# Softmax row sums of an attention block: three joins before the sum product in place of two, and its place half a group later

## The chip, the core and the metric

One core of one Trainium2 chip runs the whole kernel. The metric is device time in microseconds (us) from launch to end. Several runs are taken of each kernel, and one execution of each is profiled.

## The reference

For x of 8 batches, 1024 tokens and 512 features, in float32:

```
x = x + attention(layernorm(x))      # 16 heads of 32 features, rotary part, low-rank q and kv of rank 256
x = x + mix(layernorm(x))            # r = sigmoid(xr Wr), k = relu(xk Wk)^2, out = r * (k Wv)

attn = einsum('bhqd,bhkd->bhqk', query, key) / scale
attn = softmax(attn, axis=-1)
out  = einsum('bhqk,bhkd->bhqd', attn, value)
```

The softmax is made of exp(score - row maximum), its product with the values (o) and its row sum (l). The kernel stores o and l apart, and the mix stage divides.

## The kernel before

Three stages run one after the other: a projection (it ends at about 690 us of the trace), the attention (`attend_block`, 690 to 2360 us) and the mix stage (`mix_block`, to the end). The change lies in `attend_block` alone.

The attention runs over 32 groups (`NG`), each one batch and four heads (`HG`). A group has two halves of 512 queries (`qc`), and a half has four units (`w` = 0 to 3), each of two key tiles: `u` counts the eight units of a group, and `h = 2n + qc` counts halves. Below, w0 to w3 are the four adds of a half that belong to its units, and w0' is that of the next half.

- TensorE: eight score products of a unit (L804, into the three PSUM banks `ps_s`), between them one maximum product each for the group that comes next (L264, read by VectorE at L280 with four banks, and transposed at L259), then the value product of the unit before (L817, 16 instructions). `sums` (L831) multiplies the joined exponentials with a block of ones, so that all 128 partitions are summed. Its result takes a turn of the same three banks `ps_s`; `place`, `l_place` and `L_AT` number these turns.
- ScalarE: eight exps of a unit into `probs` (L898), a ring of `PR` = 3 units. A unit's exps wait until the value product and GpSimd's add of the unit three before are done (L893, L895). It also copies o (L873) and l (L880) out of PSUM.
- GpSimd: one add for each unit joins its two key tiles in `pairs` (L922). After w1 it issues a transfer that adds pair 0 onto pair 1 (L926, an SBUF to SBUF transfer of 1 MB that accumulates in its destination). After w3 it adds pair 2 and pair 3 itself (L929). So two buffers are left for a half, `SUMMED = [1, 3]`, and `sums` runs 2 x 4 products for them. GpSimd waits at w1 and w3 until the sum products of the half before have read the buffer.
- SyncE: in order, `load_group` for the group two ahead once the last value product of the group before is done (ten loads, 3.5 MB), the stores of o and l, and `stack_max` (L289, L290), which puts the negated maxima into the stack of the next group.
- VectorE: the maxima (L280, L283, L277) and nothing else in this stage.

The order of every queue is written out by hand with semaphores: `joined` counts landed transfers, `pair_done` GpSimd's adds (`ADDS` = 5 for a half), `sum_done` the sum products, `exped` all that ScalarE has taken out of `ps_s`.

On TensorE, `sums` of half 0 of a group stands behind the value product in unit 5, and that of half 1 in unit 1 of the next group.

Of the kernel before, what the change touches and what calls it, by code (L numbers as in the profile page):

```python
# [21 lines left out]
ALU = mybir.AluOpType  # L22
# [5 lines left out]
HD = D // H  # L28
# [645 lines left out]
def attend_block(nc, sem, held, t, att, scratch, o_d, l_d):  # L674
# [9 lines left out]
    SR = 3  # L684
    PR = 3
    ADDS = ROUNDS + 1
    SUMMED = [1, 3]
    SUMS = len(SUMMED)
    RUN = TILES + NQ
    L_AT = 2 * UT  # L690
    HALF_RUN = ROUNDS * UT + 1
    assert RUN % SR == 0 and R3 * UNITS % PR == 0

# [17 lines left out]
    with ExitStack() as ctx:  # L711
        def sb(name, shape, dt=F32):
            return ctx.enter_context(nc.sbuf_tensor(name, shape, dt))
# [3 lines left out]
        qs, ks, vt, ones = att["q"], att["k"], att["v"], att["ones"]  # L717
        loaded, v_loaded, m_scored, m_read, m_stacked = (att[k] for k in ("loaded", "v_loaded", "m_scored", "m_read", "m_stacked"))
        probs = sb("probs", [P, PR, KB, HG, CH])
        pairs = sb("pairs", [P, ROUNDS, HG, CH])  # L720
        o_sb = sb("o_sb", [P, NQ, CH])
        l_sb = sb("l_sb", [P, NQ, CH])
        ps_s = [ctx.enter_context(nc.psum_tensor(f"ps_s{i}", [P, CH], F32)) for i in range(SR)]
# [6 lines left out]
        pv_done = sem("pv_done")  # L730
        pair_done = sem("pair_done")
        joined = sem("joined")
        sum_done = sem("sum_done")
        o_out = sem("o_out")
        o_stored = [sem(f"o_stored{q}") for q in range(NQ)]
# [56 lines left out]
        @block.tensor  # L792
        def _(pe):
            def scores(n, r, u, x):
                qc, w = divmod(u, ROUNDS)
                a, kt = x % HG, w * KB + x // HG
                v = place(u * UT + x)
                if u == 0 and x == 0 and type(n) is int and n == 1:
                    pe.wait_ge(rows_set, 16 * (R3 - 1))
                if w == 0 and x == 0:  # L800
                    pe.wait_ge(m_stacked[qc], 16 * (n + 1))
                if v >= SR or not is_first(n):
                    pe.wait_ge(exped, taken(n, v - SR))
                nc.tensor.matmul(ps_s[v % SR][:, :], ks[r][:, a, kt * P:(kt + 1) * P],  # L804
                                 qs[r][:, qc, a, :], start=True, stop=True).then_inc(scored, 1)

            def pv(n, i, r, u):
                qc, w = divmod(u, ROUNDS)
                if u == 0:
                    pe.wait_ge(v_loaded[r], 16 * (i + 1))  # L810
                if w == 0 and not (is_first(n) and qc == 0):
                    pe.wait_ge(o_out, n * NQ + qc)
                pe.wait_ge(exped, taken(n, place(u * UT + UT - 1)))
                for k in range(KB):
                    kt = w * KB + k
                    for a in range(HG):
                        m = nc.tensor.matmul(ps_o[a * HD:(a + 1) * HD, :], vt[r][:, kt, a * HD:(a + 1) * HD],  # L817
                                             probs[:, (r * UNITS + u) % PR, k, a, :], start=kt == 0, stop=kt == KT - 1)
                m.then_inc(pv_done, 1)

            def sums(n, qc):

                v = l_place(n, qc)
                pe.wait_ge(exped, taken(n, v - SR))
                for k, w in enumerate(SUMMED):
                    if k == 0:
                        pe.wait_ge(joined, 16 * (n * NQ + qc + 1))
                    else:
                        pe.wait_ge(pair_done, (n * NQ + qc + 1) * ADDS)
                    for a in range(HG):  # L830
                        m = nc.tensor.matmul(ps_s[v % SR][a * HD:(a + 1) * HD, :], ones[:, :], pairs[:, w, a, :],  # L831
                                             start=k == 0, stop=k == SUMS - 1)
                    m.then_inc(sum_done, 1)

            def step(i, r, n):


                r1 = (r + 1) % R3
                i1 = i + 1 if r1 == 0 else i
                todo = [] if is_last(n) else list(range(STEPS))  # L840
                spread = SPREAD_FIRST if is_first(n) else SPREAD

                def maxima(count):
                    for _ in range(count if todo else 0):
                        max_product(nc, pe, att, ps_m, t["ident"], n + 1, r1, i1 + 1, todo.pop(0))

                for u in range(UNITS):
                    for x in range(UT):
                        maxima(spread[u][x])
                        scores(n, r, u, x)  # L850
                    if u >= 1:
                        pv(n, i, r, u - 1)
                        if u == ROUNDS + 1:
                            sums(n, 0)
                        if u == 1 and not is_first(n):
                            sums(n - 1, 1)
                    elif not is_first(n):
                        pv(n - 1, i if r else i - 1, (r - 1) % R3, UNITS - 1)
                    maxima(spread[u][UT])
                if is_last(n):  # L860
                    pv(n, i, r, UNITS - 1)
                    sums(n, 1)

            pe.wait_ge(att["ones_done"], 1)
            rounds(step)

        @block.scalar
        def _(act):
            def take_o(n, qc):
                act.wait_ge(pv_done, n * UNITS + (qc + 1) * ROUNDS)  # L870
                if not is_first(n):
                    act.wait_ge(o_stored[qc], 16 * n)
                nc.scalar.copy(o_sb[:, qc, :], ps_o[:, :]).then_inc(o_out, 1)  # L873

            def take_l(n, qc):
                v = l_place(n, qc)
                act.wait_ge(sum_done, (n * NQ + qc + 1) * SUMS)
                if not is_first(n):
                    act.wait_ge(l_stored[qc], 16 * n)
                nc.scalar.copy(l_sb[:, qc, :], ps_s[v % SR][:, :]).then_inc(exped, 1)  # L880

            def step(i, r, n):
                for u in range(UNITS):
                    if u == ROUNDS + 1:
                        take_o(n, 0)
                    if u == ROUNDS + 2:
                        take_l(n, 0)
                    if u == 1 and not is_first(n):
                        take_o(n - 1, 1)
                    if u == 2 and not is_first(n):  # L890
                        take_l(n - 1, 1)
                    if u >= PR or not is_first(n):
                        act.wait_ge(pv_done, n * UNITS + u - PR + 1)  # L893
                        qc, w = divmod(u - PR, ROUNDS)
                        act.wait_ge(pair_done, (n * NQ + qc) * ADDS + w + 1)  # L895
                    for x in range(UT):
                        act.wait_ge(scored, n * TILES + u * UT + x + 1)
                        nc.scalar.activation(probs[:, (r * UNITS + u) % PR, x // HG, x % HG, :], ps_s[place(u * UT + x) % SR][:, :],  # L898
                                             ACT.Exp, scale=SCALE).then_inc(exped, 1)
                if is_last(n):  # L900
                    take_o(n, 1)
                    take_l(n, 1)

            rounds(step)

        @block.gpsimd
        def _(pool):
            def step(i, r, n):
                for u in range(UNITS):
                    qc, w = divmod(u, ROUNDS)  # L910
                    h = n * NQ + qc
                    if not (is_first(n) and qc == 0):
                        if w == 0:
                            pool.wait_ge(joined, 16 * h)
                        elif w == 1:
                            pool.wait_ge(sum_done, (h - 1) * SUMS + 1)
                        elif w == 2:
                            pool.wait_ge(pair_done, h * ADDS)
                        else:
                            pool.wait_ge(sum_done, h * SUMS)  # L920
                    pool.wait_ge(exped, taken(n, place(u * UT + UT - 1)))
                    nc.gpsimd.tensor_tensor(pairs[:, w, :, :], probs[:, (r * UNITS + u) % PR, 0, :, :], probs[:, (r * UNITS + u) % PR, 1, :, :],  # L922
                                            ALU.add).then_inc(pair_done, 1)
                    if w == 1:
                        pool.wait_ge(pair_done, h * ADDS + 2)
                        nc.gpsimd.dma_start(pairs[:, 1, :, :], pairs[:, 0, :, :], accum_op=ALU.add).then_inc(joined, 16)  # L926
                    if w == 3:
                        pool.wait_ge(pair_done, h * ADDS + 4)
                        nc.gpsimd.tensor_tensor(pairs[:, 3, :, :], pairs[:, 2, :, :], pairs[:, 3, :, :],  # L929
                                                ALU.add).then_inc(pair_done, 1)  # L930

            rounds(step)

# [589 lines left out]
```

## Time and profile before

| | us |
|---|---|
| median of 3 runs | 3187.87 (3184.89 to 3192.63) |
| the profiled execution | 3185.31 |
| its span, first to last instruction | 3183.5 |
| mean granted TensorE clock | 0.982 |

| engine, whole span | busy us | share |
|---|---|---|
| TensorE | 3038.1 | 95% |
| VectorE | 2193.7 | 69% |
| GpSimd | 2096.1 | 66% |
| ScalarE | 1488.2 | 47% |

The shares are means over three stages. In the page's slices, GpSimd is at 9 tenths or more all through the attention and at 0 to 1 in the projection, so its 66% says little; the stage has to be read alone. In the trace PE is TensorE's matmul row and PEld its weight load, DVE is VectorE, ACT ScalarE, POOL GpSimd and SP SyncE. The records of the ones product are 16 for a half (fp32 products appear as two each).

### The profile page before, as it was taken

To read this page: it belongs to the slowest core of one execution; us is meant where nothing else is said; L and a number is where in the kernel's file an instruction comes from. 1 tells how busy PE (TensorE), PEld (TensorE's weight loads), DVE (VectorE), ACT (ScalarE), POOL (GpSimd) and SP (SyncE) were. 2 spreads that over 40 slices of the span, in tenths; PEclk is the share of its full clock that TensorE was granted. 3 is DMA by queue.
4 is the path that set the end of the run, shared out by engine and by line. 5 is a ranking of instruction groups with operands and counts; after the bars stand their busy time and mean duration, and the time that the engine had idled before them with its cause. 6 is when DMAs were issued, how large, how long until landed. Compare 5 with 4: busy or idle time off the path is not lost. (4 is left out here: it accounts for less than half of the span.)

```text
span 3183.5 us, 42900 instructions
## 1 busy us (share of the span) xinstructions
PE 3038.1 (95%) x15508; PEld 2030.9 (64%) x15508; DVE 2193.7 (69%) x3337; ACT 1488.2 (47%) x2714; POOL 2096.1 (66%) x718
## 2 busy tenths in 40 slices
PE   7999999989999999999999999999957999999998
PEld 4888888855555555555555555555515877778776
DVE  3454544568777777777777777777708787787784
ACT  1222222226666666666666666666643233233232
POOL 0111111118999999999999999999964666566663
PEclk8999999989999999999999999999988999999999
DMA  3455454655556564646455565646243223323321
GB/s 103 159 177 180 159 176 164 192 142 115 123 119 134 118 136 105 143 98 146 107 134 120 120 132 118 137 107 143 51 123 103 84 76 105 87 71 105 94 64 40
DMA packets 189068, 382.84 MB, mean 120 GB/s; under 512 B 17105, under 2 KB 53105, under 8 KB 180721
## 3 DMA queue, kind: packets, MB, share of 16 engines
q1 hardware_dynamic: 179696, 313.70, 35.8%
q0 software_dynamic: 9216, 67.11, 10.3%
q8 instruction: 93, 1.52, 0.2%
q14 instruction: 63, 0.51, 0.1%
HBM read 194.59 MB, written 118.49 MB: 98 GB/s over the span
## 5 line engine op out<-in xcount | busy, mean ns | idle before, releaser
L280 DVE TENSOR_REDUCE part_max<-ps_m 128x1 f32<-128x512 f32 x1984 | 1211.9, 681 | 362.2 <-PE ps_m L264 362.1
L922 POOL TENSOR_TENSOR pairs<-probs 128x2048 f32<-128x2048 f32 x256 | 1181.9, 4619 | 170.4 <-ACT probs L898 135.6
L898 ACT ACTIVATE probs<-ps_s 128x512 f32<-128x512 f32 x2048 | 1036.7, 625 | 324.5 <-PE ps_s L804 308.4
L264 PE MATMUL ps_m<-k_stack,q_stack 96*128 96x512 f32 x1984 | 816.0, 412 | 40.2 <-DVE neg_max L277 34.0
L804 PE MATMUL ps_s<-q_stack,k_stack 97*128 97x512 f32 x2048 | 817.0, 402 | 5.9 <-PEq L313 4.0
L264 PEld LDWEIGHTS ps_m<-k_stack,q_stack 96*128 96x128 f32 x1984 | 376.9, 190 | 306.4 <-DVE part_max L280 136.9
L817 PE MATMUL ps_o<-probs,v_tiles 128*32 128x512 f32 x4096 | 494.0, 600 | 0.0
L804 PEld LDWEIGHTS ps_s<-q_stack,k_stack 97*128 97x128 f32 x2048 | 387.7, 190 | 137.8 <-ACT probs L898 21.2
L548 POOL TENSOR_TENSOR y_cos<-y_rot,cos 64x512 f32<-64x512 f32 x16 | 20.5, 1284 | 474.6 <-DVE y_swap L644 474.6
L929 POOL TENSOR_TENSOR pairs<-pairs 128x2048 f32<-128x2048 f32 x64 | 293.2, 4581 | 5.0
L817 PEld LDWEIGHTS ps_o<-probs,v_tiles 128*32 128x32 f32 x4096 | 107.1, 109 | 231.5 <-issue 175.7
L1288 POOL TENSOR_TENSOR gate<-gate,xs 128x512 f32<-128x512 f32 x64 | 115.2, 1802 | 132.3 <-DVE diff L1354 114.7
L1208 ACT ACTIVATE relu<-mix_p 128x512 f32<-128x512 f32 x64 | 38.3, 598 | 236.6 <-PE mix_p L1106 181.6
L1104 PE MATMUL mix_p<-mix_w_o_hi,o_hi 128*128 128x512 f32 x256 | 102.9, 402 | 41.0 <-DVE o_lo L1398 28.2
L1372 DVE TENSOR_TENSOR ka_lo<-relu,ka_hi 128x512 fp32r<-128x512 f32 x64 | 104.3, 1629 | 47.9 <-ACT ka_hi L1202 45.6
L1257 POOL TENSOR_TENSOR xs<-mix_x_in,bo 128x512 f32<-128x512 f32 x64 | 117.2, 1835 | 25.7 <-DMA mix_x_in<-in_x 21.3
L831 PE MATMUL ps_s<-pairs,ones 128*32 128x512 f32 x1024 | 122.7, 596 | 5.8 <-POOL pairs L929 5.8
L880 ACT COPY l_sb<-ps_s 128x512 f32<-128x512 f32 x64 | 37.6, 587 | 183.7 <-PE ps_s L831 183.7
L1346 DVE SCALAR_TENSOR_TENSOR mixed<-diff,mu_k,xT 128x512 f32<-128x512 f32 x64 | 112.3, 1795 | 0.6
L621 DVE TENSOR_TENSOR st_v<-ps_p,bv 128x512 f32<-128x512 f32 x64 | 44.2, 691 | 98.1 <-PE ps_p L450 98.1
L1275 POOL TENSOR_TENSOR relu<-relu 128x512 f32<-128x512 f32 x64 | 68.7, 1083 | 64.4 <-ACT relu L1208 64.4
L1104 PE MATMUL mix_p<-mix_w_v_hi,ka_hi 128*128 128x512 f32 x256 | 102.5, 400 | 8.2 <-DVE ka_lo L1372 8.0
(179 smaller groups left out, 4791.8 us busy)
## 6 DMA issues: line engine op xcount, KB each, us to landing
pairs<-pairs POOLq DMA_DIRECT2D x64, 1024.0 KB, 8.0
q_stack<-q_hi_scratch SPq DMA_DIRECT2D x128, 256.0 KB, 6.2
k_stack<-k_hi_scratch SPq DMA_DIRECT2D x64, 512.0 KB, 10.8
x_in<-in_x SPq DMA_DIRECT2D x16, 1024.0 KB, 5.5
q_hi_scratch<-st_hi SPq DMA_DIRECT2D x64, 256.0 KB, 2.3
q_lo_scratch<-st_lo SPq DMA_DIRECT2D x64, 256.0 KB, 2.5
k_hi_scratch<-st_hi SPq DMA_DIRECT2D x64, 256.0 KB, 2.4
k_lo_scratch<-st_lo SPq DMA_DIRECT2D x64, 256.0 KB, 2.7
```

Of the source, the lines that this page charges most:

```text
L264: nc.tensor.matmul(bank[:, :], att["q"][r][0:ROWS, half, h, q * P:(q + 1) * P], att["k"][r][0:ROWS, h, kc * CH:(kc + 1) * CH], start=True, ...
L280: nc.vector.reduce_max(part_max[:, half, j, kc:kc + 1], bank[:, :], AX).then_inc(att["m_read"], 1)
L804: nc.tensor.matmul(ps_s[v % SR][:, :], ks[r][:, a, kt * P:(kt + 1) * P], qs[r][:, qc, a, :], start=True, stop=True).then_inc(scored, 1)
L817: m = nc.tensor.matmul(ps_o[a * HD:(a + 1) * HD, :], vt[r][:, kt, a * HD:(a + 1) * HD], probs[:, (r * UNITS + u) % PR, k, a, :], start=kt ...
L831: m = nc.tensor.matmul(ps_s[v % SR][a * HD:(a + 1) * HD, :], ones[:, :], pairs[:, w, a, :], start=k == 0, stop=k == SUMS - 1)
L898: nc.scalar.activation(probs[:, (r * UNITS + u) % PR, x // HG, x % HG, :], ps_s[place(u * UT + x) % SR][:, :], ACT.Exp, scale=SCALE).then_ ...
L922: nc.gpsimd.tensor_tensor(pairs[:, w, :, :], probs[:, (r * UNITS + u) % PR, 0, :, :], probs[:, (r * UNITS + u) % PR, 1, :, :], ALU.add).th ...
L929: nc.gpsimd.tensor_tensor(pairs[:, 3, :, :], pairs[:, 2, :, :], pairs[:, 3, :, :], ALU.add).then_inc(pair_done, 1)
L1104: nc.tensor.matmul(out, stat_hi(f), mov_hi(f), start=f == 0, stop=False)
L1257: nc.gpsimd.tensor_tensor(xs[par][:, s, :], x_in[:, s, :], bo[:, :], ALU.add).then_inc(xb_done, 1)
L1288: nc.gpsimd.tensor_tensor(gate[:, s, :], gate[:, s, :], xs[par][:, s, :], ALU.add).then_inc(out_done, 1)
L1346: v = nc.vector.scalar_tensor_tensor(mixed[:, f, :], diff[:, f, :], mu_k[:, f:f + 1], prev[:, f, :], ALU.mult, ALU.add)
```

## The change

For each half, the joins become a chain into a buffer of its own, `full`, of which there are two (`FULL`), used in turn by the halves:

- w0 writes pair 0, w1 writes into `full`, and GpSimd itself adds pair 0 onto `full` right behind w1 (it was a transfer).
- After w2 GpSimd issues a transfer that adds `pairs` 1 (the third pair) onto `full` (`joined`).
- After w0' of the next half it issues a second transfer that adds `pairs` 2 (the fourth pair) onto `full` (`filled`). It waits for `joined` before it, and at the last half it stands right behind w3.
- `sums` waits for `filled` and runs 4 products in place of 8. It stands in unit 7 (half 0) and in unit 3 of the next group (half 1), two units later than before.
- ScalarE copies l of half 0 ahead of unit 0 of the next group, and that of half 1 ahead of unit 4; SyncE's stores of l follow it. In the last group l of half 0 is copied after the last exps.
- The waits of GpSimd for `sum_done` go to one, at w1, for the half two before.

```diff
-    SUMMED = [1, 3]
-    SUMS = len(SUMMED)
+    SUMS = 1
+    FULL = 2
-    L_AT = 2 * UT
+    L_AT = 4 * UT
-        pairs = sb("pairs", [P, ROUNDS, HG, CH])
+        pairs = sb("pairs", [P, ROUNDS - 1, HG, CH])
+        full = sb("full", [P, FULL, HG, CH])
...
-                for k, w in enumerate(SUMMED):
-                    if k == 0:
-                        pe.wait_ge(joined, 16 * (n * NQ + qc + 1))
-                    else:
-                        pe.wait_ge(pair_done, (n * NQ + qc + 1) * ADDS)
-                    for a in range(HG):
-                        m = nc.tensor.matmul(ps_s[v % SR][a * HD:(a + 1) * HD, :], ones[:, :], pairs[:, w, a, :],
-                                             start=k == 0, stop=k == SUMS - 1)
-                    m.then_inc(sum_done, 1)
+                pe.wait_ge(filled, 16 * (n * NQ + qc + 1))
+                for a in range(HG):
+                    m = nc.tensor.matmul(ps_s[v % SR][a * HD:(a + 1) * HD, :], ones[:, :], full[:, (n * NQ + qc) % FULL, a, :],
+                                         start=True, stop=True)
+                m.then_inc(sum_done, 1)
...
-                        if u == ROUNDS + 1:
+                        if u == ROUNDS + 3:
                             sums(n, 0)
-                        if u == 1 and not is_first(n):
+                        if u == 3 and not is_first(n):
                             sums(n - 1, 1)
...
-                        act.wait_ge(pair_done, (n * NQ + qc) * ADDS + w + 1)
+                        act.wait_ge(pair_done, (n * NQ + qc) * ADDS + [1, 2, 4, 5][w])
...
+            def add_last_pair(h):
+                pool.wait_ge(pair_done, h * ADDS + 5)
+                pool.wait_ge(joined, 16 * h + 16)
+                nc.gpsimd.dma_start(full[:, h % FULL, :, :], pairs[:, 2, :, :], accum_op=ALU.add).then_inc(filled, 16)
...
+                    acc = full[:, h % FULL, :, :]
+                    into = [pairs[:, 0, :, :], acc, pairs[:, 1, :, :], pairs[:, 2, :, :]][w]
+                    if h >= 1:
                         if w == 0:
+                            pool.wait_ge(pair_done, h * ADDS)
+                        elif w == 1 and h >= FULL:
+                            pool.wait_ge(sum_done, h - FULL + 1)
+                        elif w == 2:
                             pool.wait_ge(joined, 16 * h)
+                        elif w == 3:
+                            pool.wait_ge(filled, 16 * h)
...
+                    if w == 0 and h >= 1:
+                        add_last_pair(h - 1)
                     if w == 1:
                         pool.wait_ge(pair_done, h * ADDS + 2)
-                        nc.gpsimd.dma_start(pairs[:, 1, :, :], pairs[:, 0, :, :], accum_op=ALU.add).then_inc(joined, 16)
-                    if w == 3:
+                        nc.gpsimd.tensor_tensor(acc, pairs[:, 0, :, :], acc, ALU.add).then_inc(pair_done, 1)
+                    if w == 2:
                         pool.wait_ge(pair_done, h * ADDS + 4)
-                        nc.gpsimd.tensor_tensor(pairs[:, 3, :, :], pairs[:, 2, :, :], pairs[:, 3, :, :],
-                                                ALU.add).then_inc(pair_done, 1)
+                        nc.gpsimd.dma_start(acc, pairs[:, 1, :, :], accum_op=ALU.add).then_inc(joined, 16)
+                if is_last(n):
+                    add_last_pair(n * NQ + NQ - 1)
```

## Rows read from the trace of the kernel before

**Rows 1.** The page, busy time of the engines over the span.

```profile
PE 3038.1 (95%) x15508; PEld 2030.9 (64%) x15508; DVE 2193.7 (69%) x3337; ACT 1488.2 (47%) x2714; POOL 2096.1 (66%) x718
```

**Rows 2.** Windows view, one group: length, PE, PEld, DVE, ACT, POOL busy, clock, DMA share, GB/s.

```profile
1466.90:1518.47 51.57, 50.46 (x292) 28.04 (x291) 39.93 (x69) 34.66 (x69) 47.65 (x13) 1.00 0.56 123
```

**Rows 3.** Waits view, that group: who waited for whom, us, times, longest.

```profile
ACT probs L898 <- PE ps_s L804: 8.6, 5, 2.4
...
POOL pairs L922 <- ACT probs L898: 2.1, 2, 1.1
...
POOL pairs L922 <- PE ps_s L831: 1.8, 3, 0.8
```

**Rows 4.** Timeline of PE, value and sum products: start, length, line, count.

```profile
1448.37 1.92 PE L817 MATMUL ps_o<-probs,v_tiles 128*32 128x512 f32 x16
...
1455.28 1.92 PE L817 MATMUL ps_o<-probs,v_tiles 128*32 128x512 f32 x16
1461.09 1.92 PE L817 MATMUL ps_o<-probs,v_tiles 128*32 128x512 f32 x16
1462.83 1.90 PE L831 MATMUL ps_s<-pairs,ones 128*32 128x512 f32 x16
1468.60 1.92 PE L817 MATMUL ps_o<-probs,v_tiles 128*32 128x512 f32 x16
```

**Rows 5.** GpSimd in the middle: timeline, and the adds of one stretch (first, last start).

```profile
1463.98 4.61 POOL L922 TENSOR_TENSOR pairs<-probs 128x2048 f32<-128x2048 f32 x1 [0.76 <-PE ps_s L831]
1468.89 0.88 POOL L926 DMA_DIRECT2D pairs<-pairs  x1 [0.30 <-POOL pairs L922]
1469.69 4.71 POOL L922 TENSOR_TENSOR pairs<-probs 128x2048 f32<-128x2048 f32 x1
...
L922 POOL TENSOR_TENSOR pairs<-probs x129: 4551/4603/4708, 1397.9 to 2223.0; 128x2048 f32<-128x2048 f32 x129
```

**Rows 6.** Timeline of GpSimd in the last group, which has no maxima.

```profile
2309.76 9.10 POOL L922 TENSOR_TENSOR pairs<-probs 128x2048 f32<-128x2048 f32 x2
2319.16 0.89 POOL L926 DMA_DIRECT2D pairs<-pairs  x1 [0.30 <-POOL pairs L922]
2319.78 9.38 POOL L922 TENSOR_TENSOR pairs<-probs 128x2048 f32<-128x2048 f32 x2
2329.23 4.56 POOL L929 TENSOR_TENSOR pairs<-pairs 128x2048 f32<-128x2048 f32 x1
2333.75 9.07 POOL L922 TENSOR_TENSOR pairs<-probs 128x2048 f32<-128x2048 f32 x2
```

**Rows 7.** Transfers from issue to landing: issued at 1494.44, at 1520.45, all 64, v load.

```profile
pairs<-pairs POOLq DMA_DIRECT2D x1, 1024.0 KB, 12.7
...
pairs<-pairs POOLq DMA_DIRECT2D x1, 1024.0 KB, 7.0
...
DMA to landing us min/median/max: 6.9/8.0/13.3
...
v_tiles<-v_scratch SPq DMA_DIRECT2D x1, 512.0 KB, 17.9
```

**Rows 8.** Load on the DMA engines: windows view (columns as Rows 2), queue of the page.

```profile
1494.00:1500.00 6.00, 6.00 (x37) 3.42 (x40) 5.08 (x9) 4.23 (x10) 5.66 (x3) 1.00 1.02 226
...
q0 software_dynamic: 9216, 67.11, 10.3%
```

**Rows 9.** Timeline of SyncE: the first of the ten loads of a group.

```profile
1482.88 0.82 SPq L242 DMA_DIRECT2D q_stack<-q_hi_scratch  x2
```

**Rows 10.** Timeline of ScalarE: last exps of unit 4, exps of unit 0.

```profile
1453.06 3.05 ACT L898 ACTIVATE probs<-ps_s 128x512 f32<-128x512 f32 x6 [0.89 <-PE ps_s L804]
...
1477.74 4.03 ACT L898 ACTIVATE probs<-ps_s 128x512 f32<-128x512 f32 x8 [2.41 <-PE ps_s L804]
```

**Rows 11.** The end of the attention: exps of unit 0 of the last group, last sum product.

```profile
2302.08 4.03 ACT L898 ACTIVATE probs<-ps_s 128x512 f32<-128x512 f32 x8 [1.61 <-PE ps_s L804]
...
2357.72 1.94 PE L831 MATMUL ps_s<-pairs,ones 128*32 128x512 f32 x8 [5.83 <-POOL pairs L929]
```

More of the change, by code:

```diff
@@ L732, in attend_block @@
         joined = sem("joined")
+        filled = sem("filled")
         sum_done = sem("sum_done")
@@ L885, in step @@
                         take_o(n, 0)
-                    if u == ROUNDS + 2:
-                        take_l(n, 0)
+                    if u == ROUNDS and not is_first(n):
+                        take_l(n - 1, 1)
                     if u == 1 and not is_first(n):
                         take_o(n - 1, 1)
-                    if u == 2 and not is_first(n):
-                        take_l(n - 1, 1)
+                    if u == 0 and not is_first(n):
+                        take_l(n - 1, 0)
                     if u >= PR or not is_first(n):
@@ L900, in step @@
                 if is_last(n):
+                    take_l(n, 0)
                     take_o(n, 1)
@@ L911, in step @@
                     h = n * NQ + qc
-                    if not (is_first(n) and qc == 0):
+                    acc = full[:, h % FULL, :, :]
+                    into = [pairs[:, 0, :, :], acc, pairs[:, 1, :, :], pairs[:, 2, :, :]][w]
+                    if h >= 1:
                         if w == 0:
+                            pool.wait_ge(pair_done, h * ADDS)
+                        elif w == 1 and h >= FULL:
+                            pool.wait_ge(sum_done, h - FULL + 1)
+                        elif w == 2:
                             pool.wait_ge(joined, 16 * h)
[L915 to L920, printed above, removed]
+                        elif w == 3:
+                            pool.wait_ge(filled, 16 * h)
                     pool.wait_ge(exped, taken(n, place(u * UT + UT - 1)))
-                    nc.gpsimd.tensor_tensor(pairs[:, w, :, :], probs[:, (r * UNITS + u) % PR, 0, :, :], probs[:, (r * UNITS + u) % PR, 1, :, :],
+                    nc.gpsimd.tensor_tensor(into, probs[:, (r * UNITS + u) % PR, 0, :, :], probs[:, (r * UNITS + u) % PR, 1, :, :],
                                             ALU.add).then_inc(pair_done, 1)
+                    if w == 0 and h >= 1:
+                        add_last_pair(h - 1)
                     if w == 1:
                         pool.wait_ge(pair_done, h * ADDS + 2)
-                        nc.gpsimd.dma_start(pairs[:, 1, :, :], pairs[:, 0, :, :], accum_op=ALU.add).then_inc(joined, 16)
-                    if w == 3:
+                        nc.gpsimd.tensor_tensor(acc, pairs[:, 0, :, :], acc, ALU.add).then_inc(pair_done, 1)
+                    if w == 2:
                         pool.wait_ge(pair_done, h * ADDS + 4)
-                        nc.gpsimd.tensor_tensor(pairs[:, 3, :, :], pairs[:, 2, :, :], pairs[:, 3, :, :],
-                                                ALU.add).then_inc(pair_done, 1)
+                        nc.gpsimd.dma_start(acc, pairs[:, 1, :, :], accum_op=ALU.add).then_inc(joined, 16)
+                if is_last(n):
+                    add_last_pair(n * NQ + NQ - 1)
             rounds(step)
```

## Prediction

> **What bounds the kernel now.** I read the page first: TensorE 95%, GpSimd 66% [rows 1]. These mix three stages, so next comes the windows view of one group in the middle of the attention: 51.57 us, of which TensorE is busy 50.46, GpSimd 47.65, VectorE 39.93, ScalarE 34.66, at a granted clock of 1.00 [rows 2]. GpSimd made 128 adds from 1397.9 to 2223.0, which is 16 groups of eight, 51.57 each [rows 5], so the pattern repeats. The waits view says who is late: ScalarE waits for score products (8.6), GpSimd for exps (2.1) and for sum products (1.8), and no row has TensorE waiting for GpSimd's sums for long [rows 3]. So TensorE's order sets the pace. But GpSimd has only 3.92 us free of 51.57.
>
> **What a sum product costs TensorE.** Value products start at 1455.28 and 1461.09, a plain unit of 5.81; with the sum products in between, the next comes at 1468.60, 7.51 later [rows 4]. The 16 records of a half cost 1.70 to 1.72, the 8 that remain 0.86. TensorE alone would need 51.57 - 2 x 0.86 = 49.85 a group.
>
> **What the change costs GpSimd.** The last group shows its pace when it never waits: the half's adds start at 2309.76, those of the next at 2333.75, so 23.99 for five adds and one transfer [rows 6]. In it the issue stands 0.30 behind the add that it waits for, and from the issue to the end of the next add pass 5.5 (1468.89 to 1469.69 + 4.71 = 1474.40) [rows 5]; adds in a row take 4.55 (9.10 / 2) [rows 6], so an issue costs 0.96 beside the 0.30. Removed: nothing, for the join that GpSimd now does after w1 takes the place of the one after w3. Added: one issue, 0.96 if it follows w0 at once (it waits for nothing that is late), 1.26 with a gap as of the other; and w0 now waits for the add right before it, 0.08 (as the join of 2329.23 stands 0.07 behind 2319.78 + 9.38 [rows 6]). So 23.99 + 0.96 + 0.08 = 25.03, at most 25.33. I take 25.15, near the lower end because the gap of 0.30 belongs to a wait that this transfer lacks. A group: 50.3 (50.06 to 50.66). That is more than TensorE's 49.85: **the bound moves to GpSimd, and most of the gain of TensorE is kept.** If adds beside a transfer run at 4.71 rather than 4.60 [rows 5], four more of them give 0.4 more, 50.9 at the top.
>
> **What the second transfer costs the sum.** The fourth pair is on its way from w0' of the next half to the sum. For half 1 that is in the time of the loads: they are issued at 1482.88 [rows 9], the last of them lands 17.9 behind its own issue [rows 7], and meanwhile the engines are full, 1.02 at 226 GB/s [rows 8]. A transfer issued there (1494.44) takes 12.7, one outside of it 7.0; the 64 lie at 6.9 to 13.3 [rows 7]. In place: exps of unit 0 end at 1477.74 + 4.03 = 1481.77 [rows 10]; w0 ends at 1486.5, landing at about 1499.3. The value product of unit 3 would start at 1448.37 + 51.57 = 1499.94 less the 1.72 that is no longer ahead of it, 1498.2, and the sum 1.74 later (as 1462.83 after 1461.09 [rows 4]), at 1500.0. Cover 0.7 us; thin, and used up by GpSimd's own lag of a few tenths. If it is gone, a loop closes: w0 4.6, transfer 12.7, wake-up 0.3, then from the sum to the add of unit 4. That add comes behind exps that end at 1456.11 [rows 10], 7.74 after the value product of 1448.37 [rows 4]; less the 1.74, plus the 0.86 and 0.14 of wake-up, 7.0. Together 24.6 to w0 of half 0, and from there GpSimd's own half of 25.15 back to the start: 49.75 a group, under 50.3. With a landing of L it is 37.05 + L, so it takes over at L = 13.25.
> For half 0 all falls outside the loads: w0' comes 24.9 after the w0 above, 29 behind the first load, lands after 7 and has 6 more to spare. The first transfer (third pair) must have landed 10.1 after its issue (w3 and w0' between: 0.96 + 2 x 4.6). In half 0 its issue falls on the last 3 us of the loads; 7.0 and at most 2 or 3 of sharing, below 10.1. The doubled traffic (10.3% of the span's engine time now [rows 8]) brings a group from 0.56 to about 0.76.
> Queues: nothing waits behind the store of l on SyncE that is needed soon. It now comes with the first and fifth unit of a group; `stack_max` behind it serves scores three units later or more. GpSimd's wait for `sum_done` (1.8 us of a group) goes, and exps (2.1) are next [rows 3].
>
> The Trainium skill, DMA: Bandwidth & Descriptors, section on queues, rings and completion order, says that a DMA engine takes turns between queues by packets. The loads of q move rows of 2 KB (512 floats), those of k and v rows of 4 KB, and by that rule the moved transfer, which meets q first, would get more of the engines and land before 12.7, perhaps after 10; no row shows a transfer beside loads of q alone. It would leave my sum as it is and makes the slower rival less likely.
>
> **The ends.** Group 0 has up to 11 maxima in a unit and one sum less for TensorE: 0.9 saved, or 0. In the last group GpSimd bounds before and after. Before: w0 at 2309.76, though the exps ended at 2302.08 + 4.03 = 2306.11 [rows 11], so 3.65 late, because the join stood ahead of it; the last sum product starts at 2357.72 [rows 11], 47.96 later. After: w0 about 0.3 late (3.35 gained); two halves to the end of w3, 50.3; the first transfer, issued 5.5 before that end, lands 7.0 after its issue, 1.5 behind it; then 0.3, the second transfer 7.0 [rows 7] and 0.1, so 59.2. Net 11.2 - 3.35 = +7.9. All behind the last sum (copy, store, barrier, mix stage) shifts as it is.
> The same page's section on the anatomy of a SWDGE transfer gives 2.0 us plus bytes by 436e3 a microsecond; for 1 MB that is an estimate of 4.4. By it this end would be 5 us shorter. The trace doesn't agree, 7.0 at the least load, and I use the 7.0.
>
> **Sum.** 30 groups (1 to 30) of 51.57 - 50.3 = 1.27: -38.1; group 0: -0.9; the end: +7.9. Together -31.1 on the profiled execution's 3185.31, thus 3154.2. That run lies 2.6 under the median of 3187.87; by the median 3156.8, and I say 3156.
>
> **The rivals** (a time is 3187.9 + 7 - 30 x (51.57 - group)).
> - TensorE still bounds: the issue overlaps the add. For it: adds that follow an issue are recorded as starting before its end [rows 5]. Group 49.85, time 3143. Chance 12%.
> - A smaller gain: landings of 13.9 to 14.3, or GpSimd slower than priced; group 50.9 to 51.3. For it: 13.3 was seen once, and three near-equal bounds (49.75, 49.85, 50.3) seldom add to their largest exactly. 3175 to 3187. Chance 17%.
> - Slower: the second transfer of half 1 lies whole under the loads, and TensorE stands at the sum of unit 3 for it in each group. The measured one of 12.7 moved its 1.05 MB in about 11 us, 0.42 of 226 GB/s; were its share a third, it would need 14 + 1.7 = 15.7. At L = 15.2 the group is 52.25 and the time 3215. It decides from L = 14.3 (group 51.34, time 3188) and shows as slower from 14.5. Against it: the measured transfer was under load for nearly all its time already, and the loads moved at the same 226. Chance 13%.
> - The change doesn't cut TensorE's work as it says (the wait on `filled` costs the weight loads their lead in each half): 0.5 a half, hidden under GpSimd's bound by all but 0.1; it changes little and lies within the forecast's range.
>
> **How the numbers follow.** The forecast (group 50.0 to 50.9, time 3148 to 3175) has 58%. Its centre is 3156. For 8 in 10 the range takes in the first rival and half of the others: 3141 to 3195. A measurement tells 0.2%, 6.4 us, from no change. Faster: 58 + 12 and most of the smaller gain, 76%. Same: 10%. Slower: 14%.
>
> **What would show it.** Right: 8 records of ones products for a half; GpSimd's halves at 25.0 to 25.4 with no idle time except at the issues; a group of 50.0 to 50.7; landings of about 12.5 and 7 for half 1 and half 0 of the second transfers; ones products waiting for the transfer or not by under 1 us; 59 us from w0 of the last group to its last sum. Wrong: landings over 13.3 and a TensorE gap of over 1 us ahead of unit 4 (the slower rival), idle time of GpSimd for exps in each half at a group of 49.9 (the first), or adds above 4.7.

## The result and the profile after

| | before | changed |
|---|---|---|
| median, us | 3187.22 | 3219.27 (3209.45 to 3225.15, 4 runs) |
| the profiled execution, us | 3185.31 | 3221.96 |
| its span, us | 3183.5 | 3220.2 |
| ratio to before | | 1.0096 (1.008 to 1.0112) |

The change makes the kernel 1% slower. The forecast was 3156 with 3148 to 3175, and the time lies outside of that, close to the 3215 of the rival called slower. The page, as far as it differs: busy time of the engines, the granted clock in 40 slices, and the queue of GpSimd's transfers.

```profile
PE 3020.7 (94%) x14996; PEld 2025.0 (63%) x14996; DVE 2205.2 (68%) x3337; ACT 1492.2 (46%) x2714; POOL 2149.1 (67%) x782
PEclk8999999989999999999999999999977999999999
q0 software_dynamic: 18432, 134.23, 20.4%
```

TensorE has 512 records less, as intended [rows 1], and the transfers doubled [rows 8]. The windows view of one ordinary group stands against [rows 2] (same columns).

```profile
1444.91:1496.15 51.24, 48.95 (x275) 27.44 (x275) 39.92 (x68) 34.67 (x69) 49.29 (x15) 1.00 0.73 165
```

TensorE is busy 1.5 us less than before, but the group is only 0.33 shorter: TensorE now idles. The waits view from 1000 to 2000 us (who waited for whom, us, times, longest) has a new row, and the timeline of TensorE shows the place of it.

```profile
PE ps_s L829 <- DMA full<-pairs: 32.2, 19, 2.8
```

```profile
1460.26 1.92 PE L819 MATMUL ps_o<-probs,v_tiles 128*32 128x512 f32 x16
1463.35 1.06 PE L829 MATMUL ps_s<-full,ones 128*32 128x512 f32 x8 [1.16 <-DMA full<-pairs]
```

This is the sum of half 1, in unit 3 of the next group. It came 1.74 us after the start of the value product before [rows 4]; now it comes 3.09 after it, because the second transfer has not landed. Of the 64 sums, those of half 0 wait for nothing, and those of half 1 wait in each of the 29 groups from 1 to 29, which have loads, 0.92 to 2.80 us, and once more at the very end. The transfers from issue to landing, for the one ahead of this sum and for all 64 second transfers:

```profile
full<-pairs POOLq DMA_DIRECT2D x1, 1024.0 KB, 14.0
...
DMA to landing us min/median/max: 6.9/7.9/15.8
```

In half 0 they land after 6.9 to 8.5 us, in the 29 groups with loads those of half 1 after 13.7 to 15.8. The transfer of before, which was issued 11.6 us behind the first load, took 12.7 [rows 7]; this one is issued 4.4 us behind it (1449.26).

**Where the time of a late transfer goes.** The queue lines of the DMA view tell when a transfer's bytes move (`q0` is the queue of GpSimd's transfers, `q1` that of the loads; then packets, MB, share of the 16 engines). First the transfer above, issued at 1449.26, in 1449.30 to 1455.50 and in 1455.50 to 1463.00:

```profile
q1 hardware_dynamic: 596, 1.37, 106.0%
...
q0 software_dynamic: 144, 1.05, 67.2%
q1 hardware_dynamic: 211, 0.78, 36.0%
```

In the 6.2 us after its issue it moves nothing at all, and then all of its 1.05 MB. The transfer of before that was issued at 1494.44, in 1494.44 to 1500.00 and in 1500.00 to 1507.50, does the same:

```profile
q1 hardware_dynamic: 342, 1.26, 101.5%
...
q0 software_dynamic: 144, 1.05, 67.2%
q1 hardware_dynamic: 225, 0.39, 15.6%
```

By the trace's packets, a transfer on free engines starts to move 1.4 to 1.5 us after its issue and moves for 5.2 us. In the kernel before, under the loads, the first packet comes after 5.6 to 6.0 us and the moving takes 6.3. In the changed kernel it comes after 6.2 to 6.7 us, and the moving takes 6.6 (medians). So most of what the loads cost a transfer is a wait ahead of its first packet; 1.1 to 1.4 us is slower moving, and the small rest lies between the last packet and the landing.

**A second loss stands in the clock.** Read from load to load (SyncE's first load of each group), the 28 full groups fall into two kinds:

| groups | length us | granted clock | landing of the second transfer, half 1 | idle ahead of the sum |
|---|---|---|---|---|
| 21 | 50.96 to 52.86, mean 51.52 | 1.00 | 13.7 to 15.8 | 0.92 to 2.80 |
| 7 | 54.80 to 56.58, mean 55.60 | 0.91 to 0.94 | 15.0 to 15.7 | 2.25 to 2.78 |

One of the seven, first TensorE's timeline, then windows of 3 us (columns as [rows 2], the clock third from the end):

```profile
1144.03 1.56 PE L829 MATMUL ps_s<-full,ones 128*32 128x512 f32 x8 [2.36 <-DMA full<-pairs]
1146.11 0.63 PE L806 MATMUL ps_s<-q_stack,k_stack 97*128 97x512 f32 x1
...
1156.31 0.40 PE L806 MATMUL ps_s<-q_stack,k_stack 97*128 97x512 f32 x1
```

```profile
1141.00:1144.00 3.00, 0.66 (x8) 0.00 (x1) 0.36 (x2) 0.00 (x0) 2.70 (x2) 1.00 0.95 234
1144.00:1147.00 3.00, 2.97 (x12) 1.38 (x13) 0.65 (x1) 0.73 (x2) 3.00 (x2) 0.58 1.11 314
1147.00:1150.00 3.00, 2.63 (x7) 1.59 (x6) 1.79 (x5) 1.61 (x3) 2.09 (x1) 0.50 1.02 213
1150.00:1153.00 3.00, 3.00 (x8) 2.32 (x7) 2.52 (x4) 1.98 (x5) 0.00 (x0) 0.50 0.18 36
```

TensorE stands for 2.36 us, then it is granted 0.50 of its clock (1.2 of 2.4 GHz) for some 10 us (6.8 us in four of the seven groups), and a score product lasts 0.63 in place of 0.40. Both groups of idle time over 2.25 us that kept the clock at 1.00 (idle 2.80 and 2.47) took 52.86 and 52.84 us. So the idle time alone costs under 3 us, and the lower clock another 2.3 to 4, 3.1 in the mean.

**The end** is as the prediction had it. GpSimd's timeline, w2 of successive halves, and the last transfer and sum:

```profile
2299.10 4.61 POOL L928 TENSOR_TENSOR pairs<-probs 128x2048 f32<-128x2048 f32 x1
...
2324.28 4.61 POOL L928 TENSOR_TENSOR pairs<-probs 128x2048 f32<-128x2048 f32 x1
...
2329.81 9.52 POOL L928 TENSOR_TENSOR pairs<-probs 128x2048 f32<-128x2048 f32 x2
...
2387.02 0.89 POOL L910 DMA_DIRECT2D full<-pairs  x1 [2.45 <-DMA full<-pairs]
```

```profile
2394.12 1.93 PE L829 MATMUL ps_s<-full,ones 128*32 128x512 f32 x8 [13.72 <-DMA full<-pairs]
```

A half of GpSimd that never waits takes 25.18 (2324.28 - 2299.10; 25.15 was forecast). w0 of the last group starts at about 2334.7, the last sum 59.4 later (59.2 was forecast).

**The sum of it.** Span +36.7: 28 groups of 52.54 against 51.57 give +27.1; before them -1.3; from the last first load to the last sum 163.45 against 152.84, +10.6 (one wait with a lowered clock in it). Within the 27.1, the 21 groups give -1.1; the seven would give +6.5 at 52.5 us (what their landings cost at full clock) and give 21.7 more with the clock. This is the split of the one profiled execution (3221.96); how many groups lose the clock in the others (3209.45 to 3225.15) is not known.

### The profile page after: what moved, and what is told of

It is laid out like the page before. It is cut to its first block and busy times, and to the rows that moved or that the text cites. A ratio compares the mean times of both kernels' runs of the same rounds, so it can differ in the third digit from the quotient of the medians.

```text
span 3220.2 us, 42003 instructions
## 1 busy us (share of the span) xinstructions
PE 3020.7 (94%) x14996; PEld 2025.0 (63%) x14996; DVE 2205.2 (68%) x3337; ACT 1492.2 (46%) x2714; POOL 2149.1 (67%) x782
## 5 line engine op out<-in xcount | busy, mean ns | idle before, releaser
L928 POOL TENSOR_TENSOR pairs<-probs 128x2048 f32<-128x2048 f32 x192 | 897.7, 4675 | 126.2 <-ACT probs L896 123.7
L264 PE MATMUL ps_m<-k_stack,q_stack 96*128 96x512 f32 x1984 | 828.5, 419 | 38.0 <-DVE neg_max L277 31.5
L806 PE MATMUL ps_s<-q_stack,k_stack 97*128 97x512 f32 x2048 | 829.9, 408 | 6.0 <-PEq L313 4.1
L264 PEld LDWEIGHTS ps_m<-k_stack,q_stack 96*128 96x128 f32 x1984 | 383.4, 193 | 311.1 <-DVE part_max L280 157.0
L806 PEld LDWEIGHTS ps_s<-q_stack,k_stack 97*128 97x128 f32 x2048 | 395.5, 193 | 143.8 <-ACT probs L896 25.5
L928 POOL TENSOR_TENSOR full<-probs 128x2048 f32<-128x2048 f32 x64 | 302.7, 4730 | 19.7 <-ACT probs L896 19.7
L934 POOL TENSOR_TENSOR full<-pairs,full 128x2048 f32<-128x2048 f32 x64 | 293.6, 4587 | 5.0
L1381 DVE TENSOR_TENSOR ka_lo<-relu,ka_hi 128x512 fp32r<-128x512 f32 x64 | 112.9, 1764 | 47.9 <-ACT ka_hi L1211 45.6
L829 PE MATMUL ps_s<-full,ones 128*32 128x512 f32 x512 | 71.0, 626 | 62.3 <-DMA full<-pairs 62.3
```

What stands on the lines that cost most here:

```text
L264: nc.tensor.matmul(bank[:, :], att["q"][r][0:ROWS, half, h, q * P:(q + 1) * P], att["k"][r][0:ROWS, h, kc * CH:(kc + 1) * CH], start=True, ...
L928: nc.gpsimd.tensor_tensor(into, probs[:, (r * UNITS + u) % PR, 0, :, :], probs[:, (r * UNITS + u) % PR, 1, :, :], ALU.add).then_inc(pair_d ...
L934: nc.gpsimd.tensor_tensor(acc, pairs[:, 0, :, :], acc, ALU.add).then_inc(pair_done, 1)
L1381: nc.vector.tensor_tensor(ka_lo[:, g, :], relu[:, g % RELU, :], ka_hi[:, g, :], ALU.subtract).then_inc(kal_done, 1)
```

## The experiments

All ratios are to the kernel before on the same chip (3192.86 us for the first four, 3186.16 for the last three). The changed kernel was not measured again beside them, so comparisons with it go by the ratios. The code shown is cut to the lines that matter; `...` marks what is left out.

**The sum one unit later.** The turns of the banks (`L_AT`, `place`, `l_place`) and the copy of l move with it.

```diff
-                        if u == 3 and not is_first(n):
+                        if u == 4 and not is_first(n):
                             sums(n - 1, 1)
...
-                    if u == ROUNDS and not is_first(n):
+                    if u == ROUNDS + 1 and not is_first(n):
                         take_l(n - 1, 1)
```

> The changed kernel, but the sum product of half 1 stands one unit later (unit 4 of the next group in place of unit 3), so that its transfer has 5.8 us more. Theory A (the transfer of the fourth pair lands too late under the loads, 13.7 to 15.8 us after its issue, and TensorE stands at this sum): the idle time of 0.9 to 2.8 us ahead of the sums goes, the clock stays at 1.00 in all groups, GpSimd bounds with 50.3 us a group (50.0 to 50.7), landings stay at 14 to 15.5, time 3150 to 3165. Theory B (three near-equal bounds meet and GpSimd with its second issue can't do better than 51.5): the group stays at 51.3 to 51.7 even with the idle time gone, time 3185 to 3195.

Measured: 3156.68 us, ratio 0.9889 (0.9873 to 0.9906). The clock is 1.00 in all groups. Windows view of one group, and the landings of the second transfers:

```profile
1456.27:1506.19 49.92, 48.81 (x275) 27.54 (x275) 39.91 (x68) 34.65 (x69) 48.27 (x15) 1.00 0.76 167
```

```profile
DMA to landing us min/median/max: 6.9/8.4/16.0
```

The transfers are as slow as ever, and they no longer matter. Theory A holds and B falls. The 28 groups have a mean of 50.13. They show how the two bounds lie together: most groups take TensorE's 49.92 (the sum of half 1 waits for nothing in them), but GpSimd's issue after w0 slips by 0.33 a group against the loads (from 3.6 to 9.9 us after the first of them), so it needs about 50.25. When the slip has used up the extra unit, TensorE waits once more (1.12 to 1.40 us), and the group takes 51.3 to 51.5; that happens three times.

The slip also shows that the distance from the first load is not what sets the landing. A second transfer that is issued 9.2 us behind it in this run still lands after 14.1, although 11.6 us gave 12.5 in the kernel before. By then GpSimd's first transfer of the half has come to lie beside the loads of q, the last of which lands 14.5 us behind the first load here and 9.3 in the changed kernel. So the second transfer meets q again.

**Loads of almost nothing.**

```diff
+    w = CH if n < R3 else 16
...
-            sp.dma_start(att["q"][r][part * HD:(part + 1) * HD, qc, :, :].bitcast(F32),
-                         src[n, :, qc * CH:(qc + 1) * CH].rearrange("(a p) t -> p a t", p=HD)).then_inc(att["loaded"][r], 16)
+            sp.dma_start(att["q"][r][part * HD:(part + 1) * HD, qc, :, 0:w].bitcast(F32),
+                         src[n, :, qc * CH:qc * CH + w].rearrange("(a p) t -> p a t", p=HD)).then_inc(att["loaded"][r], 16)
...
```

> The changed kernel, but from group 3 on the ten loads of a group bring only the first 16 columns (v: the first key tile), so the products run over stale data; the order and the waits are the same. Theory A (the loads stretch the transfer): it lands after 7 to 8 us in all groups, no idle time ahead of the sums of unit 3, clock 1.00, group 50.3 us (50.0 to 50.7), time 3150 to 3165. Theory B (GpSimd or TensorE bound near 51.5 whatever the transfer does): group over 51.2, time over 3180.

Measured: 3155.29 us, ratio 0.9882 (0.9862 to 0.9902). Landings:

```profile
DMA to landing us min/median/max: 6.9/7.0/9.2
```

No sum of unit 3 waits until GpSimd's slip has grown to 10 us, the clock is 1.00 in all 28 groups, and most groups take 49.9 us (mean 50.06). The kernel computes with stale data; only its times count. With the sum at its place in unit 3 and free DMA engines, the forecast's time comes out. It was the loads that kept the transfer from landing in time.

**Filler ahead of the wait.**

```diff
+                for x in range(5 if filler is not None else 0):
+                    nc.tensor.matmul(ps_s[v % SR][:, :], ks[filler][:, 0, x * P:(x + 1) * P],
+                                     qs[filler][:, 0, 0, :], start=True, stop=True)
                 pe.wait_ge(filled, 16 * (n * NQ + qc + 1))
...
-                            sums(n - 1, 1)
+                            sums(n - 1, 1, r)
```

> The changed kernel, with five score-like products of 0.233 us each (1.17 us together) into the free bank ahead of the wait of the sum in unit 3, whose result is overwritten. They fill part of TensorE's idle time. Theory A (in the groups of 54.8 to 56.6 us the idle time of 2.25 us and more brings the granted clock down to its lower level for the next few us, and that costs about 4 us a group): idle time is at most 1.7 us, the clock stays at 1.00 in all groups, the groups are 51.0 to 52.3, time about 3190 (28 us less than the changed kernel). Theory B (the clock falls for another reason, such as the load on the chip as a whole): as many groups of under 0.95, time 3215 to 3225 or more.

Measured: 3201.7 us, ratio 1.0027 (1.0017 to 1.0037), so 0.7% or 22 us less than the changed kernel by the ratios (18 by the medians, which were not taken side by side), for more work. The landings are the same (up to 16.1). The longest but one wait, and its group:

```profile
1815.05 1.07 PE L832 MATMUL ps_s<-full,ones 128*32 128x512 f32 x8 [1.44 <-DMA full<-pairs]
```

```profile
1794.97:1847.85 52.88, 50.31 (x280) 28.26 (x280) 39.91 (x68) 34.66 (x69) 49.25 (x15) 1.00 0.71 160
```

With a landing of 15.7 this group takes 52.88 at a clock of 1.00. The changed kernel had 56.49 for the same landing, at 0.91. All 28 groups are at 1.00 and between 51.30 and 53.09, mean 51.77. Theory A holds: the waits are shorter and no group loses the clock. One rival is left open, since the changed kernel was not measured beside this run: that the clock would not have fallen here in any case. Against it stands the trace of the changed kernel itself, where the clock fell behind eight of its ten waits of 2.25 us and more and behind none of the 19 shorter ones, and the last run below, where it fell behind waits of 3.44 and 3.74 on another chip than this run's. By the ratios, the gain fell 6 us short of the 28 expected, since the filler is no longer hidden where the landing is early: 51.37 where the changed kernel had 51.04.

**The loads in another order.**

```diff
-    for part, src in enumerate((qh_d, ql_d, qh_d)):
...
     for part, src in enumerate((kh_d, kh_d, kl_d)):
...
     sp.dma_start(att["v"][r][:], v_d[n]).then_inc(att["v_loaded"][r], 16)
+    for part, src in enumerate((qh_d, ql_d, qh_d)):
...
```

> The changed kernel, with the loads of a group in the order k, v, q in place of q, k, v. Theory A1 (the moved transfer is slower than the 12.7 us of before because it meets the 2 KB rows of q first, where that of before met the 4 KB rows of k and v): landings fall to about 12.7, the sum of unit 3 waits under 0.3 us, group 50.3, time about 3155. Theory A2 (it is slower because it lies under the loads for its whole way, whichever they are): landings stay at 13.7 to 15.8, time 3210 to 3225.

Measured: 3169.54 us, ratio 0.9926 (0.9907 to 0.9946). Landings of the second transfers:

```profile
DMA to landing us min/median/max: 6.9/8.0/13.9
```

In half 1 they are 11.8 to 13.9 with a median of 13.1, where the changed kernel has 13.7 to 15.8 with a median of 14.3. So most of what the moved transfer lost against the 12.7 of before is due to the loads of q that it meets first (A1); about 0.4 us is not. The first packet now comes after 5.5 to 6.0 us, as in the kernel before, and no longer after 6.2 to 6.7. That the length of q's rows is the reason, and not something else in which these loads differ, is not shown; only the order was changed. Nor does a run tell why some landings are over a microsecond longer than the others in every kernel. A1 gave 3155, but 13.1 is still late for the sum in unit 3: it waits 0.26 to 1.82 us in 18 groups, and these take 50.3 to 51.9.

**The kernel before with half of the sum products.**

```diff
-    SUMMED = [1, 3]
+    SUMMED = [3]
```

> The kernel before, but the sum products run over one of the two buffers only (4 products in place of 8, waits for both as before), so l lacks the first two pairs; the copy of l adds 1.0 so that no sum is zero. GpSimd's work is that of the kernel before. If TensorE bounds the kernel before and a sum costs it 0.86 us per four products, the group falls from 51.57 to 49.85 us, GpSimd stays below with 48.0, and the time is 3187 - 30 x 1.72 = 3135 (3130 to 3142), ratio about 0.983. If the kernel before is held by a mix of TensorE and GpSimd, the group stays over 50.5 and the time over 3155.

Measured: 3138.95 us, ratio 0.9843 (0.9826 to 0.9859).

```profile
1460.11:1510.01 49.90, 48.77 (x275) 27.54 (x275) 39.93 (x68) 34.68 (x69) 47.67 (x13) 1.00 0.56 128
```

The group is 49.90 (49.85 was worked out), and 49.88 to 49.98 in all of them. TensorE bounds the kernel before, and leaving out half of the sum products is worth 1.67 us a group or 1.6% of the time. This is the most that the change could have brought.

**The last half without transfers.** The kernel of the later sum, and in `sums`:

```diff
+                if is_last(n) and qc == NQ - 1:
+                    h = n * NQ + qc
+                    for k, (count, buf) in enumerate(((3, full[:, h % FULL, :, :]), (4, pairs[:, 1, :, :]), (5, pairs[:, 2, :, :]))):
+                        pe.wait_ge(pair_done, h * ADDS + count)
+                        for a in range(HG):
+                            m = nc.tensor.matmul(ps_s[v % SR][a * HD:(a + 1) * HD, :], ones[:, :], buf[:, a, :],
+                                                 start=k == 0, stop=k == 2)
...
```

> The kernel of the later sum (e1_sum_later), but the very last half has no transfers: TensorE sums its three buffers itself with 12 products, four of them behind the last add. In e1_sum_later the last add ends at 2314.65 and the last sum starts at 2323.86. Theory (the two transfers of 7 us in a row are what the end costs): that stretch shrinks to under 1 us and one issue less stands ahead of it, so 10 us less than e1_sum_later, about 3146, ratio to before 0.986. Rival (the mix stage waits for something else, its weights or its input, and not for the last sum): no change, 3156, ratio 0.989.

Measured: 3145.73 us, ratio 0.9864 (0.9847 to 0.988): 0.25% or 8 us less than the later sum alone by the ratios, 11 by the medians. The intervals of the two ratios overlap, so the traces decide: from the last first load to the last sum product it is 153.2 us in place of 163.5. The theory holds. TensorE's timeline at the end:

```profile
2308.01 1.03 PE L832 MATMUL ps_s<-full,ones 128*32 128x512 f32 x8
2310.95 1.06 PE L832 MATMUL ps_s<-pairs,ones 128*32 128x512 f32 x8 [1.92 <-POOL pairs L937]
2315.42 1.94 PE L832 MATMUL ps_s<-pairs,ones 128*32 128x512 f32 x8 [3.40 <-POOL pairs L937]
```

The last sum starts 0.06 behind the last add (2306.36 + 9.00). This is the best kernel of the study, 1.4% faster than before and 2.3% faster than the changed one.

**Both together with the other order of the loads.** The kernel above with the loads of groups 3 and up as k, v, q.

> As e6_sum_later_end, and the loads of groups 3 and up in the order k, v, q. In e4_q_last this order brought the landings from 13.7 to 15.8 us down to 11.8 to 13.9. With the sum one unit later the landing is no longer waited for, except in the few groups where GpSimd's lag has grown; GpSimd bounds at 50.2 us a group either way. Expected: the same as e6_sum_later_end within 3 us. If the landing still mattered, it would be 5 us or more faster.

Measured: 3170.73 us (3160.53 to 3180.07), ratio 0.9944 (0.9927 to 0.996). A miss by 25 us: shorter landings make this kernel slower. The first 15 groups take 49.9 as in the one above. GpSimd's timeline in the 16th:

```profile
1510.19 0.88 POOL L956 DMA_DIRECT2D full<-pairs  x1 [0.30 <-POOL pairs L947]
1510.81 9.59 POOL L947 TENSOR_TENSOR pairs<-probs 128x2048 f32<-128x2048 f32 x2
1524.30 0.88 POOL L929 DMA_DIRECT2D full<-pairs  x1 [3.90 <-ACT probs L915]
```

GpSimd slips by 0.33 a group against the loads. Here it slipped until its first transfer of half 1 was issued 0.1 us behind the first load (at 1510.11) and no longer ahead of it. It landed after 13.6 in place of 7 to 10, at 1523.8, and GpSimd stood 3.90 us before it could issue the second (the row names the exps, but w0 had used these and ended at 1520.40; what the issue still waits for is `joined`), TensorE stood 3.74 at the sum, and the group took 55.90:

```profile
1538.55 1.06 PE L848 MATMUL ps_s<-full,ones 128*32 128x512 f32 x8 [3.74 <-DMA full<-pairs]
```

There are four such groups (55.5 to 58.2 us, clock 0.91 to 0.97). In one of them, from 1717.01 to 1772.54, the clock is lower though the sum of half 1 waits for nothing. The delay reaches TensorE through the exps, as two shorter stretches of idle time close together:

```profile
1736.29 0.50 PE L274 MATMUL ps_m<-k_stack,q_stack 96*128 96x512 f32 x1 [0.75 <-DVE neg_max L287]
...
1738.52 0.80 PE L816 MATMUL ps_s<-q_stack,k_stack 97*128 97x512 f32 x1 [1.26 <-ACT probs L915]
```

```profile
1735.50:1738.50 3.00, 1.01 (x4) 0.49 (x3) 2.03 (x4) 0.63 (x2) 2.92 (x2) 0.86 1.06 228
1738.50:1741.50 3.00, 2.98 (x7) 2.41 (x8) 1.40 (x3) 2.49 (x5) 3.00 (x1) 0.50 1.11 240
```

So the longest single wait does not tell alone whether the clock falls. In the kernel of the order q, k, v the late second transfer stops TensorE for 1.1 to 1.4 us each time that the slip comes near 10 us, which takes the slip back to between 8.3 and 9.0. That the short waits there are what saves it is read from the two traces; no run takes them away alone.

## Why the prediction was wrong

- **Removed work: right.** 0.86 us for four products; 49.85 was forecast for TensorE alone, 49.90 was measured with half of the sums, 49.92 with the later sum.
- **GpSimd's added issue: right.** 25.15 a half forecast, 24.97 to 25.18 measured in the last halves; 0.96 for an issue that follows an add at once is what the timeline shows. The bound at 50.3 a group is about the 50.25 that GpSimd needs in the later sum, where the groups have a mean of 50.13 and the ratio is 0.9889 (0.990 was forecast). But that is a kernel whose transfer is hardly waited for.
- **The second transfer: this step failed.** The loop through the transfer was drawn rightly, 37.05 + L, and the 21 groups at full clock follow it: 51.04 for L = 13.8, 51.24 for 14.0, 52.84 for 15.3; they lie -0.3 to +0.5 from it, most of them 0.2 to 0.3 above. The term that was mis-sized is L. I took the 12.7 of a transfer issued 11.6 us behind the first load, when only loads of k and v were still on their way, and carried it to one issued 4 us behind. There it meets the loads of q, and lands after 13.7 to 15.8, 14.3 in the median. The loop takes over at 13.25 by the prediction's own working, and at 14.3 the whole gain is gone: the 3156 assumed 50.3 a group, but without any loss of clock the group is about 51.77 (the filler run, ratio 1.0027), 1.47 x 30 = 44 us more.
- **The picture of a shared transfer: wrong.** The rival called slower was priced by a share, as if the transfer had moved for about 11 us with 0.42 of the 226 GB/s. The rows of the two kernels show a wait of 6 us without a byte and then 6.3 to 6.6 us of moving, against 5.2 on free engines.
- **The clock: not in the forecast at all.** The rival for "slower" was priced at full clock; in seven groups TensorE's idle time brought it to the lower level, 3.1 us more in each. It is most of the loss against the kernel before: 1.0096 with it, 1.0027 with the filler. That the median of 3219.27 is close to the rival's 3215 is in part luck: a landing of 14.3 in place of its 15.2, and 22 us of clock.
- **The rule on turns by packets spoke the wrong way.** I had read from it that the transfer would get more of the engines beside the small rows of q and land after perhaps 10. It landed later: 14.3 beside q, 13.1 beside k and v. The Trainium skill, DMA: Bandwidth & Descriptors, section on queues, rings and completion order, may be right on the turns, but the traces show that the transfer has no turn at all for the first 6 us, and only then moves beside the loads; what it waits for there no run shows.
- **The first transfer: right.** Below 10.1 in half 0 was forecast, 7.8 to 9.3 was measured in the groups with loads (10.6 in the first group, whose units are longer), and nothing waited for it but the second transfer of the very last half.
- **The ends: right**, 59.4 against 59.2.
- **The lead of the weight loads**, the small rival, isn't told apart: it may be part of the 0.2 to 0.3 by which most groups lie above 37.05 + L.
- **The chances.** Three ways of equal length within 1% (TensorE 49.85, transfer 49.75, GpSimd 50.3) deserved more than 13% for the one whose price was carried over from another place.

## What to carry to other kernels

When a change puts a transfer on the way to a product, price it by a row of a transfer that meets the same other traffic, and if there is none, give the cover in microseconds beside the spread of the landings: 0.7 us of cover against a spread of 2 us isn't cover. Look also at when its bytes move: a transfer that waits 6 us ahead of its first packet is not one that moves slowly. The sum was needed by nobody soon, so its place was free: one unit later turned +1.0% into -1.1%. A wait on TensorE must be priced with the clock that it may cost, and a filler helps to tell the two apart.

## What the hardware showed

- An accumulating transfer of 1 MB within SBUF lands after 6.9 to 9.2 us with next to no loads beside it (the run with small loads), 11.6 to 14.5 where it meets loads of k and v first (the kernel before, and the two runs with q last), and 13.6 to 16.1 where it meets those of q first.
- Under the loads such a transfer as a rule moves nothing for the first 5.5 to 6.8 us after its issue, and then moves for 6.3 to 6.6 us (medians); on free engines these are 1.4 to 1.5 and 5.2 us.
- Idle time of TensorE of 2.25 to 2.8 us ahead of a sum was followed in eight cases of ten by a granted clock of 0.50 for 3.4 to 10.2 us; a single wait at a sum of up to 1.8 us never was, in this kernel, with the filler and with q last. In the last run, two stretches of 0.75 and 1.26 us within 3 us of each other were followed by it too.
- With one engine 0.3 us a group slower than another, the slip is harmless for 15 groups and then crosses the start of a burst of loads. A mean over groups hides it; the length group by group shows it.
